# An attention and low-rank FFN kernel: one normalising pass a tile, and x added in the last stage by GpSimd

## The reference

```python
x = x + _L0_xattn_ref(_layernorm(x), ctx_512, ctx_512)
x = x + _L0_ffn_ref(_layernorm(x), select_weight, ...)
# attention: 32 query heads, 8 key/value heads of width 32
scores = jnp.einsum('bkgsd,bktd->bkgst', qh, kh) / scale
out = jnp.einsum('bkgst,bktd->bkgsd', jax.nn.softmax(scores, axis=-1), vh)
# ffn: eight gates for each row; the largest selects a low-rank update
return (1.0 - sel_scale) * x + sel_scale * mod_x_bias
```

## Time and profile before

| | us |
|---|---|
| median of three runs | 1024.54 |
| lowest and highest | 1022.45, 1025.27 |
| span of the profiled execution | 1023.9 |

### The profile page before, as it was taken

How to read it: one execution, slowest core, us unless ns; L and a number is a source line. 1 busy time by engine, 2 the same in 40 slices (tenths; PEclk the granted TensorE clock), 3 DMA queues, 4 the chain that set the end, 5 groups by cost and what they waited for, 6 DMA issues and landing times.

```text
span 1023.9 us, 24706 instructions
## 1 busy us (share of the span) xinstructions
PE 949.4 (93%) x9518; PEld 372.5 (36%) x9518; DVE 904.8 (88%) x1138; ACT 761.3 (74%) x1333; POOL 794.4 (78%) x422
## 2 busy tenths in 40 slices
PE   4789999999999999999999999999999999999996
PEld 3223233333333232333333333332222226777773
DVE  6869999999999999999999999998888876888976
ACT  7468888888888888888888888888777777554440
POOL 7158999999999999999999999998999998222110
PEclk9989999999999999999999999999999999999998
DMA  7675677767677767676767686766555744766423
GB/s 247 184 167 114 161 154 168 156 162 159 155 158 167 168 152 170 145 171 150 180 143 175 138 188 134 182 122 154 119 119 139 165 95 141 247 213 236 148 104 164
DMA packets 319876, 164.19 MB, mean 160 GB/s; under 512 B 182216, under 2 KB 307240, under 8 KB 319760
## 3 DMA queue, kind: packets, MB, share of 16 engines
q1 hardware_dynamic: 319456, 161.76, 64.3%
q0 software_dynamic: 304, 0.85, 0.3%
HBM read 107.58 MB, written 54.53 MB: 158 GB/s over the span
## 4 chain that ended last, share of the span: by engine, by line
PE 36%; DVE 30%; issue 25%; ACT 5%; POOL 2%; DMA 1%; SPq 0%; DVEq 0%; POOLq 0%; ACTq 0%
DVE row_max L949 14%; PE psum L589 8%; PE psum L603 6%; PE psum L616 5%; PE psum L734 5%; DVE den_t L961 4%; PE psum L551 4%; ACT probs L884 3%; PE psum L712 3%; DVE o_t L955 3%; PE psum L577 2%; DVE probs L1161 2%; DVE prod_mem L1008 2%; PE psum L700 1%; ACT prod_mem L824 1%
## 5 line engine op out<-in xcount | busy, mean ns | idle before, releaser
L884 ACT ACTIVATE probs<-psum 128x512 f32<-128x512 f32 x1024 | 554.7, 596 | 106.7 <-PE psum L589 88.7
L949 DVE TENSOR_REDUCE row_max<-psum 128x4 f32<-128x2048 f32 x248 | 566.0, 2282 | 63.5 <-PE psum L551 63.1
L589 PE MATMUL psum<-q_stack,k_stack 97*32 97x512 f16 x4096 | 335.0, 386 | 10.2 <-issue 3.6
L363 POOL TENSOR_TENSOR sums<-probs 128x2048 f32<-128x2048 f32 x63 | 287.8, 4568 | 19.5 <-ACT probs L884 19.5
L351 POOL TENSOR_TENSOR sums<-probs 128x2048 f32<-128x2048 f32 x63 | 287.2, 4558 | 10.2 <-PE psum L626 5.5
L603 PE MATMUL psum<-probs,v_in 128*32 128x512 f32 x2048 | 268.9, 598 | 1.0
L589 PEld LDWEIGHTS psum<-q_stack,k_stack 97*32 97x32 f16 x4096 | 96.8, 95 | 258.7 <-ACT probs L884 148.6
L551 PE MATMUL psum<-high_mem 32*128 32x512 f16 x992 | 98.3, 385 | 23.7 <-DVE row_max L949 20.0
L323 POOL TENSOR_TENSOR o_t<-o_t,inv 128x512 f32<-128x512 f32 x64 | 67.1, 1048 | 44.2 <-DVE inv L967 44.2
L328 POOL TENSOR_TENSOR o_all<-o_all,o_t 128x512 f32<-128x512 f32 x64 | 81.5, 1274 | 9.5 <-POOL o_t L323 0.4
L603 PEld LDWEIGHTS psum<-probs,v_in 128*32 128x32 f32 x2048 | 59.4, 111 | 61.1 <-issue 16.7
(11 more groups left out here) (120 smaller groups left out, 788.9 us busy)
## 6 DMA issues: line engine op xcount, KB each, us to landing
q_stack<-q_split SPq DMA_DIRECT2D x192, 128.0 KB, 3.4
xa<-in_x_dram SPq DMA_DIRECT2D x32, 512.0 KB, 4.7
o_all<-in_x_dram SPq DMA_DIRECT2D x256, 64.0 KB, 2.5
x_attended<-o_all SPq DMA_DIRECT2D x64, 256.0 KB, 4.1
out_dram<-probs SPq DMA_DIRECT2D x32, 512.0 KB, 2.9
q_split<-prod_mem SPq DMA_DIRECT2D x15, 1024.0 KB, 5.4
xa<-x_attended SPq DMA_DIRECT2D x16, 512.0 KB, 4.5
probs<-x_attended SPq DMA_DIRECT2D x16, 512.0 KB, 5.3
```

What stands on the lines that cost most here:

```text
L363: pool.tensor_tensor(sums[:, 2 * u % SUMS], probs[:, u % 2, 0], probs[:, u % 2, 1], ALU.add).then_inc(front_done, 1)
L589: last = pe.matmul(st_ps[row:row + D, bank_of["score", u, n], :], k_stack[:, u % SLOTS, t * P + row:t * P + row + D], q_stack[:, u % SLOTS ...
L884: act.activation(probs[:, s, keys, g, :], st_ps[:, bank_of["score", u, n], :], ACT.Exp, scale=EXP_SCALE).then_inc(exped, 1)
L949: dve.reduce_max(row_max[:, u % 2, t:G * ST:ST], s_ps[:], AX.X).then_inc(reduced, 1)
```

## The change

ACT normalises a tile in one pass, in place, `normalise_tile`: scale is the root, bias is the mean times the root, negated. POOL makes that bias by one more small operation behind each root; DVE's `neg_mean` goes. The x ring has four tiles in place of two and a second buffer `xn`.

In the units, POOL's `normalise` writes `o_t` times `inv` straight into `o_all`, one pass where there were two, and the 256 loads of x into `o_all` go. In their place x is loaded by tiles of 512 KB (`load_addend(n)`, through two buffers in `prod_mem` for tiles 0 to 5, then three in `tail_mem`), and POOL adds it to `xa` (`add_x(n)`, 128x1024): tiles 0 to 5 in units 57 to 62, 6 and 7 between row roots, the others each ahead of the row root of the tile two before. `row_moments` waits for `added`.

```diff
-            CENTRE_AT = (13, NSC)
+            NORM_AT = 13
@@ inverse_root
+                    pool.wait_ge(rstd_done, 2 * n + 1)
+                    pool.tensor_scalar(neg_mean[:, k:k + 1], mv[:, k, 0:1], rstd[:, k:k + 1], -1.0,
+                                       ALU.mult, ALU.mult).then_inc(rstd_done, 1)
@@ normalise (POOL)
-                    pool.tensor_tensor(turned_rows, turned_rows,
+                    if h == 0:
+                        wait(pool, a_out[half], 64 * (u // KV))
+                    pool.tensor_tensor(o_all[:, half, :, h, :], o_t[:, u % 2].rearrange("p (a d) -> p a d", d=D),
                                        inv[:, u % 2].unsqueeze(2).to_broadcast([P, S // D, D]),
-                                       ALU.mult).then_inc(o_scaled, 1)
-                    wait(pool, xo_in[half], 16 * G * HALF * (u // KV + 1))
-                    wait(pool, o_scaled, u + 1)
-                    pool.tensor_tensor(o_all[:, half, :, h, :], o_all[:, half, :, h, :], turned_rows,
-                                       ALU.add).then_inc(o_made, 1)
+                                       ALU.mult).then_inc(o_made, 1)
+                def add_x(n):
+                    q, k, t = n // ST, n // ST % GROUPS, n % ST
+                    pool.wait_ge(t_in[ST * k + t], 16 * (q // GROUPS + 1))
...
+                    pool.tensor_tensor(attended, attended, x_addend(n).rearrange("p (h g d) -> p g h d", h=KV, g=G),
+                                       ALU.add).then_inc(added, 1)
@@ POOL, loop over u and behind it
                     if u == UNITS + 1:
                         row_root(1, 1, 0)
+                        add_x(SOON)
                         row_root(1, 1, 1)
+                        add_x(SOON + 1)
...
+                    if 0 <= u - 1 - (UNITS - KV) < SOON:
+                        add_x(u - 1 - (UNITS - KV))
...
                 for n in range(ST + 2, TILES):
+                    if n + 2 < TILES:
+                        add_x(n + 2)
                     row_root(n // ST, n // ST % GROUPS, n % ST)
@@ SP
+                        if n < SOON:
+                            load_addend(n)
...
+                        if ST * (q + EARLY) + t < TILES:
+                            load_addend(ST * (q + EARLY) + t)
...
+                        for n in range(SOON, EARLY * ST):
+                            load_addend(n)
@@ ACT
-                def centre(n):
-                def scale_centred(n):
+                def normalise_tile(n):
+                    act.wait_ge(rstd_done, 2 * n + 2)
+                    act.activation(x_tile(n), x_tile(n), ACT.Identity, scale=rstd[:, n % 2:n % 2 + 1],
+                                   bias=neg_mean[:, n % 2:n % 2 + 1]).then_inc(xn_done, 1)
...
+                        act.wait_ge(added, SOON)
...
-                            if t == ST - 1 and u % 2 == 1:
-                                centring_pass()
@@ DVE
-                    dve.tensor_scalar(neg_mean[:, k:k + 1], mv[:, k, 0:1], -1.0, None, ALU.mult)
-                    wait(dve, t_in[ST * k + t], 16 * (q // GROUPS + 1))
+                    dve.wait_ge(added, n + 1)
```

More of the change, by code:

```diff
@@ L113, in xattn_ffn @@
             o_all = sb("o_all", [P, 2, S // D, HALF, D], f32)
[L114 removed]
+            x_ring = xa_early[EARLY - 1]
             cin = sb("cin", [P, 2, CE], f32)
@@ L142, in xattn_ffn @@
             mixT = tail_mem[:, 0, ST * E:ST * E + ST * P].rearrange("p (t m) -> p t m", t=ST)
+            x_late = as_tiles(tail_mem[:, 0, ST * E + ST * P:ST * E + ST * P + 3 * E])
+            x_soon = as_tiles(prod_mem[:])
+            SOON = 6
+            x_addend = lambda n: x_soon[:, n % 2] if n < SOON else x_late[:, (n - SOON) % 3]
             y = as_tiles(prod_mem[:])
@@ L162, in xattn_ffn @@
             a_out = [sem("a_out0"), sem("a_out1")]
-            xo_in, o_scaled = [sem("xo_in0"), sem("xo_in1")], sem("o_scaled")
+            add_in, added = [sem(f"add_in{i}") for i in range(5)], sem("added")
             max_scored, reduced, max_turned = sem("max_scored"), sem("reduced"), sem("max_turned")
@@ L423, in store_half, with load_addend @@
                                      ).then_inc(a_out[half], 16)
[L425 to L429, removed]
-                        cols = slice(((half * HALF + h) * G + g) * D, ((half * HALF + h) * G + g + 1) * D)
-                        sp.dma_start(o_all[g * D:(g + 1) * D, half, :, h, :],
-                                     x[b, :, cols].rearrange("(a c) d -> c a d", c=D)).then_inc(xo_in[half], 16)
+                def load_addend(n):
+                    if n < SOON:
+                        slot = n % 2
+                        wait(sp, added, n - 1)
+                    else:
+                        slot = 2 + (n - SOON) % 3
+                        if n >= SOON + 3:
+                            sp.wait_ge(added, n - 2)
+                    sp.dma_start(x_addend(n), x[n // ST, n % ST * P:(n % ST + 1) * P, :]).then_inc(add_in[slot], 16)
                 for n in range(FIRST + 1):
@@ L469, in _ @@
                         store_half(u - 3)
-                    if live(u + 1):
-                        for g in ((1,), (2, 3), (), (0,))[u % HALF]:
-                            load_addend((u + 1) // HALF, g)
                     if live(u) and u % 2 == 0 and n + 2 < TILES:
@@ L828, in _ @@
                 high_part(0, 0)
-                centre(0)
-                scale_centred(0)
-                centre(1)
-                for i in range(1, PIECES):
-                    high_part(0, i)
-                for n in range(1, FIRST):
-                    high_part(n, 0)
-                    scale_centred(n)
+                normalise_tile(0)
+                for n in range(FIRST):
+                    if n > 0:
+                        high_part(n, 0)
                     if n + 1 < FIRST:
-                        centre(n + 1)
+                        normalise_tile(n + 1)
                     for i in range(1, PIECES):
                         high_part(n, i)
-                centre(FIRST)
                 def normalise(q, k, t):
@@ L854, in _ @@
                     tile = tile_of(u)
-                    def centring_pass():
-                        if u % 2 == 0 and whole(tile):
-                            scale_centred(tile)
-                        if u % 2 == 1 and whole(tile + 1):
-                            centre(tile + 1)
                     for t in range(ST):
@@ L869, in _ @@
                             copy_constants()
-                        if t == ST - 1 and not live(u):
-                            centring_pass()
+                        if t == ST - 1 and u == -AHEAD:
+                            normalise_tile(tile)
                         if live(u):
@@ L880, in _ @@
                                     make_shift(u + 1)
-                                if n == CENTRE_AT[u % 2]:
-                                    centring_pass()
+                                if n == NORM_AT and u % 2 == 0 and whole(tile):
+                                    normalise_tile(tile)
                                 wait(act, scored, NSC * u + n + 1)
@@ L985, in variance @@
                     dve.wait_ge(stats_done, n + 1)
-                    wait(dve, xn_done, n - 1)
+                    wait(dve, rstd_done, 2 * (n - 1))
                     dve.bn_aggr(mv[:, n % 2], stats[:, n % 2]).then_inc(mv_done, 1)
```

20 lines of the change are left out of this document (6 added, 14 removed).

## The result

| | us |
|---|---|
| before, median of four runs | 1024.9 (1022.45 to 1025.28) |
| changed kernel, median of four runs | 1064.32 (1061.04 to 1065.09) |
| ratio, 95% interval | 1.0392 (1.037 to 1.0414) |
| profiled execution: time, span | 1061.04, 1059.2 |

The change costs 39 us. Forecast were 1045 and a range up to 1059: the sign was right, the size was not, and the time lies outside the range. The profiled execution is the fastest of its four, so its span is only 35.3 us above that of the kernel before, and the last 4 us of the 39 are not divided here. Four stretches make up the 35.3: the start, to the loop's steady part, -5.95; from there to the first `finish` 21.9 (it starts at 879.88 before, 9.67 us ahead of the row at 889.55 in the earlier trace rows, and at 895.87 after, 16.0 later); the first three groups of the last stage 9.5 (58.0 us became 67.5); the rest 9.8.

What follows compares the result with a forecast made beforehand. Bounds: a DVE-PE chain in the loop, POOL in the seam (837 to 876 us), PE in the last stage. 1023.9 -1 -2 +0 +15.3 +2.5 +2 +4 = 1044.7, say 1045 us; range 1029 to 1059.

Steps and rivals of the forecast that it cites:

- The loop: Attention loop: removing ACT's pass is covered by its wait for PE, pair stays 25.3 us; 0 (0 to -2).
- The start: First units: tile 4 normalised before its wait, -1 (0 to -2); addend loads ahead of a key store go, -2.
- The second term: Start, near 63 us: four addend loads SP issued ahead of the key store go; -2 us (0 to -3.4).
- the price of a restart in the seam: Seam, after PE idles some 13 us: lower granted clock costs PE's work +2.5 us (0 to 4).
- The lag on GpSimd: Units 57 to 62 and seam: x adds make POOL's last sum 4 us later, last normalise +3.5 us (1.5 to 5).
- the 1.7 us of waits "that are absorbed": Seam: about 1.7 us of POOL's waits for DVE were taken off the lateness of the last normalise.
- The queue: Seam: SP issues tile 8's addend late, its add stands before root 6; +15.3 us (11 to 19), earlier POOL lag included.
- PE's hole: Seam, near 878 us: PE, in order behind tile 6, idles some 13 us.
- The ring: Last stage: result, addend load, add, root just fits at 5 us landing; third transfer lengthens landing, +2 us (0 to 4).
- The exclusion: Last stage: long POOL adds and DVE's small gate operations exclude each other, half hidden; +4 us (0 to 12).
- locked gates: Rival, last stage: every add blocks the gate chain for its length; 29 us unhidden, 1057 with half hidden; chance 0.14.
- the groups of 20 to 21 us: Sign that the forecast is right: last-stage groups take 20 to 21 us in place of 19.3.

Runs made afterwards that it cites:

- the two edits at the start: Kernel before with one normalising pass a tile, and the first four x loads queued behind the store of tiles 4 and 5: 1018.8 us.
- both edits of the order: Changed kernel with the addend of tile 8 issued early and each row root ahead of the add of the tile two later: 1051.5 us.
- 1061.1: Changed kernel with the addend of tile 8 issued with those of tiles 6 and 7, ahead of the last half batch's store: 1061.1 us.
- 1040.6: The 1061.1 kernel with adds of 64 of the 1024 columns from tile 8 on, all loads kept: 1040.6 us.
- 1051.5: Changed kernel with the addend of tile 8 early and each row root ahead of the add of the tile two later: 1051.5 us.
- 1031.4: The 1051.5 kernel with adds of 64 columns from tile 8 on, all loads kept: 1031.4 us.
- 1054.2: The 1061.1 kernel with full adds but no loads of x from tile 9 on: 1054.2 us.
- 1025.0: Changed kernel, addend of tile 8 early, with adds of 64 columns from tile 8 on and no x loads from tile 9 on: 1025.0 us.
- 1053.1: The 1051.5 kernel with full adds but no loads of x from tile 9 on: 1053.1 us.
- 1029.5: The 1053.1 kernel with each add from tile 8 on replaced by a memset of 2048 columns and an add of 128 columns: 1029.5 us.

## Why the prediction was wrong

Point by point, in the order of its terms.

**The loop: right.** A pair lasts as long as before, with one pass less on ScalarE and one on GpSimd.

**The start: too small in the profile.** -3 forecast, -5.95 between the two profiles, just outside its two terms' ends (-5.4). By medians the two edits at the start give 4.3, which is inside. The second term had -2 with -3.4 as its end; an early `row_max` (at 36.02 us before) comes 1.1 us earlier, and between it and the loop another 4.8 us go. PE's clock stays at 1.00 at 64 to 68 us, where it was 0.50. The prediction knew that row, and used it only as the price of a restart in the seam, not as something that would go away here.

**The lag on GpSimd: right to the last sum (3.9 of 4), then too small.** 6.6 instead of 3.5 at the last `normalise`. What failed in this term is the 1.7 us of waits "that are absorbed": GpSimd waited 2.91 us for VectorE's moments of tile 5, and the exclusion works in both directions already here. VectorE's own sum took 5.50 us (2.25 in the earlier trace rows): it was held until GpSimd's last sum ended at 847.0, and then ran. The row of the changed kernel:

```profile
843.67 5.50 DVE L1045 TENSOR_TENSOR sums<-probs 128x2048 f32<-128x2048 f32 x1
```

VectorE's second sum, at 849.74 by that, then held the last operation of the first root, 2.09 us in place of 0.27. ScalarE and PE wait for that root: PE idles 4.56 us ahead of its first turns, at 853.61, and these take 3.24 us in place of 2.05. The denominators, VectorE's moments of tile 5 and root 5 stand behind them and come 5.7 us late.

**The queue: right in itself.** 14.7 us from `normalise` to root 6 (13.7 forecast); to the first `finish` 21.9 in all, 17.8 forecast. The 4.1 between are the lag (3.1), the queue (1.0) and a gate operation of 2.29 us at 889.00 (2.1 too long), which is 2 us too much; where those came back the rows do not settle. PE's hole, some 13 us in the forecast, was 12.91. But the experiments show that this hole is no sum of its own: with order and loads mended and long adds kept, the first `finish` still comes at 888.19, and both edits of the order gave back 12.8 us and not 17.8.

**The ring: right.** +2 forecast over five groups; with short adds and all loads it is 146.0 us from the first `finish` to the end, against 144.0 in the kernel before, and the load's landing, 7 us, does not break it. With long adds it does: at 942.22 a load of 7.64 us leads to an add of 2.35, a root, and gates that VectorE starts after a wait of 3.73 us.

**The exclusion: the step that failed.** +4 with 12 as its upper end; measured 20.1 to 29.2, by four pairs of runs that differ in the length of the adds (1061.1 - 1040.6, 1051.5 - 1031.4, 1054.2 - 1025.0) or in what GpSimd does in its place (1053.1 - 1029.5). The mechanism was named, both ways and for the right operations, but "half of the delay lies under PE's work" was an assumption without a row. The groups counted above show that none of it does. The sum was too small even by its own words: two adds a group, 2.4 us each, six groups and half of it hidden are 14.4 us, and the prediction gives no reason for writing 4. In the kernel before PE already waits for that `finish`, so the gate chain has no slack there. PE in order of time, kernel before:

```profile
910.66 1.96 PE L734 MATMUL psum<-down,probs 128*128 128x512 f32 x4 [0.52 <-DVE probs L1161]
```

One or two hits a group, of 0.9 to 2.2 us, go to the end in full, and after most of the long idle times PE's next four matmuls run at the lower clock. The rival "locked gates" had it at 14.5 net, 29 if nothing is hidden; it had the mechanism, a chance of 0.14, and still too low a time (1057), since it took half of the delay as hidden as well. The prediction's sign for that rival, small VectorE operations of 1 to 2.4 us, came true beside its own signs of the hole; the groups of 20 to 21 us did not (21.6 to 23.6).

Together, in profiled times: 1044.7, and 2.95 less for the start, 4.1 more for the seam, 13.3 more for the last stage (19.3 where the ring and the exclusion had 6), gives 1059.2.

What stays open: why long adds cost 29 us with one order and no loads, and 20 with loads. In the rows the adds meet different VectorE operations from run to run, which would do it; no run was made to control that, so it is not shown.

## What to carry to other kernels

Before work moves to GpSimd, look at what VectorE does at that time. Engines do not wait for one another by semaphores only. Here a chain of small operations with two SBUF inputs paid for each long GpSimd read that it met, up to the length of the GpSimd instruction, and cutting the reads into four pieces only spread the hits. Ask for each hit whether the chain has slack there: a row in which the next engine already waits for that chain says that it has none. And where a queue is mended at one tile, read at which tile the same wait comes back.

## What the runs showed of the hardware

- VectorE waits for GpSimd as well as the other way round: 5.50 us for a sum of 2.25, and 1.6 to 2.4 for operations of 0.19. Of small GpSimd operations, one of 0.27 us took 2.09 beside VectorE's sum.
- A memset on GpSimd leaves two-input VectorE operations alone (0.42 beside it), but holds a TENSOR_SCALAR of 0.18 us for 1.65. The `finish` behind that is not held, ScalarE's reader of the result is. Behind another held TENSOR_SCALAR (1.46 us) a TENSOR_REDUCE of 0.18 us took 1.39.
- After an idle time of PE of 3.71 us (the granted clock read 1.00 during part of it) four matmuls took 3.49 us at 0.50 (1.2 of 2.4 GHz). After 2.61 us of idling they took 1.96, but after 2.24 us 2.88: the one wait alone doesn't tell what follows it.
